# Second attention: the maxima leave from SyncE's queue, the inverse one step later, the last normalisation behind its masks

## What is computed

```python
def _L0_attn_b_ref(encodings, attn_w, attn_b, out_w, out_b):
    qkv = encodings @ attn_w.T + attn_b
    qkv = qkv.reshape(b, n, 16, 3 * 8).transpose(0, 2, 1, 3)
    q, k, v = jnp.split(qkv, 3, axis=-1)
    mask = jnp.arange(n)[:, None] <= jnp.arange(n)[None, :]
    scores = jnp.einsum('bhki,bhqi->bhkq', k, q) / math.sqrt(8)
    scores = jnp.where(mask, scores, -10000.0)
    probs = jax.nn.softmax(scores, axis=2)
    combined = jnp.einsum('bhkq,bhkl->bhql', probs, v)
    out = combined.transpose(0, 2, 1, 3).reshape(b, n, 128)
    return out @ out_w.T + out_b
```

## Time and profile before

| | us |
|---|---|
| median of 3 runs | 768.71 (766.55 to 768.84) |
| the profiled execution, its own time | 768.21 |
| its span, first to last instruction | 766.4 |
| PE busy in the span | 685.7 (89%) |
| DVE, ACT, POOL busy | 484.8, 454.9, 431.0 |
| second attention, block 0 to block 7 | about 348 to 573 |

### The profile page before, as it was taken

One profiled execution on the slowest core, in us unless ns is written; L12 is line 12 of the kernel. 1 busy time (PEld: TensorE's weight loads), 2 busy tenths in 40 slices (PEclk: granted clock), 3 DMA queues, 4 the chain that ended last, 5 costly groups with the idle time before them and its releaser, 6 DMA issues.

```text
span 766.4 us, 13977 instructions
## 1 busy us (share of the span) xinstructions
PE 685.7 (89%) x4706; PEld 472.0 (62%) x4706; DVE 484.8 (63%) x957; ACT 454.9 (59%) x801; POOL 431.0 (56%) x444
## 2 busy tenths in 40 slices
PE   3789896799999999999999999999878899999996
PEld 1455555477787777665555555555445777777784
DVE  6668885567555586456767767766658356675510
ACT  2677774555665565445656566666665555556663
POOL 4455441377867776433444544543555677777763
PEclk9999998899999999999999999999999999999998
DMA  6110320000000003531645654645111000000000
GB/s 182 39 38 20 62 27 2 0 1 1 0 1 0 0 0 99 177 111 43 209 147 177 239 169 156 229 140 180 57 63 41 16 15 15 14 0 15 15 15 27
DMA packets 33028, 52.47 MB, mean 68 GB/s; under 512 B 4560, under 2 KB 9680, under 8 KB 32976
## 3 DMA queue, kind: packets, MB, share of 16 engines
q1 hardware_dynamic: 32784, 51.53, 21.3%
q10 hardware_dynamic: 192, 0.26, 0.1%
HBM read 27.15 MB, written 24.38 MB: 67 GB/s over the span
## 4 chain that ended last, share of the span: by engine, by line
PE 48%; DVE 13%; POOL 13%; issue 12%; ACT 8%; DMA 5%; ACTq 1%; POOLq 1%; DVEq 0%; SPq 0%
PE banks L220 44%; POOL f_h_lo L1122 5%; POOL f_g_lo L1129 5%; ACT b_prob L1448 2%; DMA b_o_dram<-b_o 2%; DVE xn L182 2%; DVE a_mx L645 2%; PE banks L212 2%; ACT a_prob L548 1%; DMA b_den<-b_o_dram 1%; DVE a_prob L657 1%; DVE f_hidden L1072 1%; DVE a_straight L630 1%; PE banks L957 1%; DVE f_gate L1068 1%
## 5 line engine op out<-in xcount | busy, mean ns | idle before, releaser
L1129 POOL TENSOR_TENSOR f_g_lo<-f_gelu,f_g_hi 128x512 fp32r<-128x512 f32 x128 | 167.9, 1316 | 68.8 <-ACT f_g_hi L1024 68.5
L1023 ACT ACTIVATE f_gelu<-banks,cols 128x512 f32<-128x512 f32 x128 | 88.2, 689 | 141.9 <-PE banks L220 139.3
L220 PE MATMUL banks<-f_g_hi,whi 128*128 128x512 f32 x320 | 132.7, 415 | 15.1 <-POOL f_g_lo L1129 15.1
L1534 DVE TENSOR_REDUCE b_segment_max<-banks 128x6 f32<-128x768 f32 x128 | 116.2, 949 | 45.0 <-PE banks L220 44.6
L1644 POOL TENSOR_SCALAR_AFFINE_SELECT b_prob<-b_prob 128x512 f32<-128x512 f32 x128 | 81.7, 641 | 111.6 <-ACT b_prob L1448 111.4
L1448 ACT ACTIVATE b_prob<-banks 128x768 f32<-128x768 f32 x128 | 102.6, 809 | 63.4 <-PE banks L220 55.0
L220 PE MATMUL banks<-f_g_lo,whi 128*128 128x512 f32 x320 | 128.1, 400 | 0.0
L1122 POOL TENSOR_TENSOR f_h_lo<-f_hidden,f_h_hi 128x512 fp32r<-128x512 f32 x60 | 77.5, 1292 | 58.7 <-DVE f_h_hi L1075 58.7
L220 PE MATMUL banks<-f_h_hi,whi 128*128 128x512 f32 x256 | 104.4, 408 | 3.2 <-POOL f_h_lo L1122 2.7
L220 PE MATMUL banks<-f_h_lo,whi 128*128 128x512 f32 x256 | 102.1, 399 | 0.0
L1024 ACT ACTIVATE f_g_hi<-banks,cols 128x512 fp32r<-128x512 f32 x128 | 87.1, 680 | 0.0
(11 more groups left out here) (124 smaller groups left out, 1052.1 us busy)
## 6 DMA issues: line engine op xcount, KB each, us to landing
f_h_hi<-b_q_dram SPq DMA_DIRECT2D x16, 512.0 KB, 4.0
f_h_lo<-b_k_dram SPq DMA_DIRECT2D x16, 512.0 KB, 5.0
b_o_dram<-b_o SPq DMA_DIRECT2D x8, 1024.0 KB, 4.3
b_q_dram<-b_q_hi SPq DMA_DIRECT2D x16, 256.0 KB, 3.2
b_k_dram<-b_k_hi SPq DMA_DIRECT2D x16, 256.0 KB, 3.3
w_stage<-in_wF SPq DMA_DIRECT2D x8, 352.0 KB, 3.2
b_q_dram<-b_q_lo SPq DMA_DIRECT2D x8, 256.0 KB, 3.4
b_k_dram<-b_k_lo SPq DMA_DIRECT2D x8, 256.0 KB, 3.8
```

The source lines that it names most:

```text
L220: return nc.tensor.matmul(out, lhsT, rhs, start=start, stop=stop)
L1023: nc.scalar.activation(gf[c % 2][:, :], z_bank[c % 2], ACT.Gelu, scale=scale).then_inc(s_gf, 1)
L1129: nc.gpsimd.tensor_tensor(lo[:, c, :], gf[c % 2][:, :], hi[:, c, :].bitcast(F32), ALU.subtract).then_inc(s_glo[c % 2], 1)
L1534: nc.vector.reduce_max(seg[:, g, s, 2 * p:2 * p + 2, :], first_pass[:, 2 * p:2 * p + 2, 0:3 * P].rearrange("p b (c k) -> p b c k", c=3), A ...
```

## The change

act_max keeps the negation and loses its two waits and its DMA. SP sends the maxima instead. Those of half 1 of block b go out in sp_out, between the loads of b_oT and b_den and the wait for the inverse (in block 0, which has no sp_out, before sp_rows). Those of half 0 of block b+1 go out in sp_rows, between the loads of half 0 and those of half 1 (in block 6, which has no sp_rows, behind sp_out). The very first go out before block 0. DVE's inverse moves from step 2 to step 3. In block 7 the normalisation of block 6 moves behind all of that block's masks.

```diff
-            INVERSE_AT = 2
+            INVERSE_AT = 3
@@ act_max
                 nc.scalar.activation(nmT[half][:, :], misc[0:2 * GROUPS, :], ACT.Copy, scale=-1.0).then_inc(s_nm, 1)
-                act.wait_ge(s_nm, HALVES * m.t + half + 1)
-                act.wait_ge(s_p1, STEPS * m.t + HALF * (half + 1))
-                act.dma_start(qs[m.odd][3 * DB::QUART, 2 * half:2 * half + 2, :].bitcast(F32), nmT[half][:, :].bitcast(F32))\
-                    .then_inc(s_ml[half][m.odd], 16)
@@ pool_body
-                    if before and n == OUT_AT:
+                    if before and one and n == OUT_AT:
                         pool_normalise(pool, b.after(-1))
...
+                if not one:
+                    pool_normalise(pool, b.after(-1))
@@ sp_rows
                 for half in range(HALVES):
+                    if half and between:
+                        between()
                     if not fresh:
                         sp.wait_ge(s_p2, v["used"][half])
@@
+            def sp_max(sp, m, half, v):
+                sp.wait_ge(s_nm, v["negated"])
+                sp.dma_start(qs[m.odd][3 * DB::QUART, 2 * half:2 * half + 2, :].bitcast(F32), nmT[half][:, :].bitcast(F32))\
+                    .then_inc(s_ml[half][m.odd], 16)
@@ sp_out
                 sp.dma_start(den[:, :], view[:, DB, :].rearrange("h (c t) -> h c t", t=DEN_COLS)).then_inc(s_ol, 16)
+                if between:
+                    between()
                 sp.wait_ge(s_inv, v["read"])
@@ sp_body
                 if before:
-                    sp_out(sp, b.after(-1), out_at)
+                    sp_out(sp, b.after(-1), out_at, send_max)
+                else:
+                    send_max()
                 if two:
-                    sp_rows(sp, b.after(2), rows_at, False)
+                    sp_rows(sp, b.after(2), rows_at, False, send_next_max)
+                elif one:
+                    send_next_max()
```

More of the change, by code:

```diff
@@ L1701, in rows_values, with sp_rows @@
                         "used": [value(sp, UNITS * (n.t - 2) + UNITS // HALVES * (half + 1)) for half in range(HALVES)]}
-            def sp_rows(sp, n, v, fresh):
+            def sp_rows(sp, n, v, fresh, between=None):
                 if not fresh:
@@ L1725, in sp_rows, with max_values @@
                             .then_inc(s_ld[half][n.odd], 16)
+            def max_values(sp, m, half):
+                return {"negated": value(sp, HALVES * m.t + half + 1)}
+            def sp_max(sp, m, half, v):
+                sp.wait_ge(s_nm, v["negated"])
+                sp.dma_start(qs[m.odd][3 * DB::QUART, 2 * half:2 * half + 2, :].bitcast(F32), nmT[half][:, :].bitcast(F32))\
+                    .then_inc(s_ml[half][m.odd], 16)
             def out_values(sp, b):
@@ L1729, in out_values, with sp_out @@
                         "read": value(sp, b.t + 1)}
-            def sp_out(sp, b, v):
+            def sp_out(sp, b, v, between=None):
                 sp.wait_ge(s_oc, v["copied"])
@@ L1748, in sp_body, with send_max, send_next_max @@
                 rows_at = rows_values(sp, b.after(2)) if two else None
+                max1_at = max_values(sp, b, 1)
+                max0_at = max_values(sp, b.after(1), 0) if one else None
+                def send_max():
+                    sp_max(sp, b, 1, max1_at)
+                def send_next_max():
+                    sp_max(sp, b.after(1), 0, max0_at)
                 if before:
-                    sp_out(sp, b.after(-1), out_at)
+                    sp_out(sp, b.after(-1), out_at, send_max)
+                else:
+                    send_max()
                 if two:
-                    sp_rows(sp, b.after(2), rows_at, False)
+                    sp_rows(sp, b.after(2), rows_at, False, send_next_max)
+                elif one:
+                    send_next_max()
             def sp_program(sp):
@@ L1757, in sp_program @@
                     sp_rows(sp, n, rows_values(sp, n), True)
+                sp_max(sp, FIRST_BLOCK, 0, max_values(sp, FIRST_BLOCK, 0))
                 sp_body(sp, FIRST_BLOCK, False, True, True)
```

## The result

The changed kernel takes 778.39 us in the median of four runs (777.32 to 782.86), the kernel before 767.85 (766.55 to 768.84) in the same comparison: a ratio of 1.0156, with a 95% interval of 1.0128 to 1.0183. It is slower, by 10.5 us. The forecast was 770.9, with a range up to 776.0; the time lies outside it.

What follows compares the result with a forecast made beforehand. PE, busy for 89% of the span, was taken as the bound, with SP's chain setting the period after. Blocks -0.7 + 1.8 - 1.8 - 0.7 = -1.4, plus 3.6 for clock falls, gave +2.2: 770.9 us, range 763.5 to 776.

Steps and rivals of the forecast that it cites:

- The freed ACT: Steps 0 and 5: without ACT's DMA issue PE gains 0.45 and 0.80, 1.25 us a block, 29.06 to 27.8.
- The deciding term, SP's chain: Blocks 1 to 5: the later inverse delays the row loads; period 29.4, +1.8 us over five blocks.
- The maxima: Half 0's maxima, sent behind the k load at block starts: 0 to 0.7 us a block, taken as 0.
- The clock: Half clock after PE's waits at starts of blocks 2 to 6: 1.2 us in three of five, +3.6, bounds 0 and 6.
- Blocks 6 and 7: The last two blocks: block 6 loads no rows and gains 1.8 us; block 7 gains 0.7.
- The maxima come last: Rival: PE waits at block starts for maxima, not k rows; 0.4 to 0.7 a block, 773 to 774.4; chance 0.17.
- No clock falls: Rival: same chain, but waits too short or wrongly placed for falls; -1.4, 767.3 us; chance 0.32.
- short chain everywhere: Rival: every block gets block 3's 13.25 us chain; period 28.67, -5.2, 763.5 us; chance 0.10.
- the inverse is hidden: Rival: SP's chain after the inverse is under 12.4 us, so no wait; -9.5, 759.2 us; chance 0.03.
- The normalisation behind the masks: Block 7: masks of step 7 no longer wait behind the normalisation; gain 0.4 us.

Runs made afterwards that it cites:

- e1: The changed kernel with the inverse put back after step 2, SP still sending the maxima and the last normalisation behind its masks: 763.64 us, ratio 0.9937.
- e5: The kernel before with SP sending the maxima and nothing else changed (inverse in step 2, last normalisation ahead of its masks): 762.77 us, ratio 0.996.
- e2: The kernel before with only the inverse moved to step 3, ACT still sending the maxima: 774.49 us, ratio 1.0106.
- e6: The changed kernel with the inverse's store and load on SP between the stores of q and those of k: 764.28 us, ratio 0.9967.
- e3: The changed kernel with the maxima of half 0 sent ahead of both loads of half 0: 778.81 us, ratio 1.0156.
- e9: e5 with the maxima of half 1 sent right behind the issue of the output's store: 762.97 us, ratio 0.9959.
- e10: e9 with the last block's normalisation behind its masks, as in the change: 764.08 us, ratio 0.9972.
- e8: The changed kernel with one extra matmul, its result unused, at the start of step 0 of blocks 1 to 6: 771.91 us, ratio 1.0059.
- e4: The changed kernel with SP holding back the loads of half 1 until the next block's step 0 has made its second scores: 782.49 us, ratio 1.0151.

## Why the prediction was wrong

**The freed ACT: right in kind and about right in size.** 1.25 us a block were forecast, a period of 27.8 without other limits. From first pass to first pass e1 and e5 show 28.0 in the mean of blocks 1 to 5: 27.2 to 27.6 in blocks 2 to 4, and 28.8 to 29.4 in blocks 1 and 5, behind which PE still waits for SP's transfers (in e1 0.7 and 1.0 us).

**The deciding term, SP's chain: right in kind, too small.** The forecast said that PE would wait at each block's start, with the chain through the inverse as the cause. It does, and e2 and e6 show that cause: the inverse alone makes the wait, and taking the stores of q out from behind it removes 14.1 us. From the first pass to the inverse's store I had 13.88. After, it is 13.97 in block 1 and 13.44 in block 5, and 14.9 to 16.2 where the clock fell in between: right. From the inverse's store to the next first pass I had 1.47 + 14.0 + 0.07 = 15.54. After, the five blocks have 17.13, 16.17, 16.08, 15.39 and 16.42, mean 16.24: **0.70 short a block, 3.5 in five**.

Half of the 0.70 is the inverse's own store: in blocks 1 and 5 the load went out 2.56 and 2.19 us behind it, in place of the 1.47 that I used for all, which is 0.36 in the mean of five. From that load to the landing of the k rows it was 14.20 in place of 14.0, and from there to the first pass 0.21 in place of 0.07.

What stands beside the small store where it is slow can be seen in the view of DMA queues. It has one more queue in blocks 1 (386 to 390 us) and 5 (510.9 to 513.1) than in block 2 (418 to 421), where the store took 1.45:

```profile
q8 instruction: 1, 0.02, 2.0%
...
q8 instruction: 1, 0.02, 2.8%
```

That is a transfer of 16 KB on the queue that the profile calls instruction, begun 0.08 and 0.16 us behind the issue of the store. In the 13 traces other than e6 the inverse is stored 104 times. All 15 stores that took over 1.6 us (1.67 to 3.13) had such a transfer under way, and of the 89 that took 1.45 or so, one had, for its first 0.2 us. In e6 the two slowest, 4.05 and 3.88, had one too, and the three at 2.2 to 2.3 had none.

In e2, with ACT as the sender, the mean to the next first pass is 15.78; 0.18 of its 0.24 is the same thing, in one block. Leaving out the slow stores, the change is 0.34 over the forecast and e2 0.06, so by this comparison of two single traces SP's sending of the maxima costs about 0.28 a block. The longer stores have the instruction transfers beside them and aren't counted to it.

**The maxima: the wrong end of a range.** I had 0 to 0.7 a block and took 0, "as they are 16 KB beside 512". The chain shows these 16 KB landing 4.25 us after their issue: size doesn't help behind 1 MB of rows. The measured 0.28 lies below the middle of the range. Of it PE feels about half directly: only in blocks 3 and 6 did it start the first pass later than the k rows' landing allows, by 0.14 and 0.50, which is 0.13 in the mean of five. By e3 it can't be had back by sending them first: then the k rows go out later and come last.

By the rule of the Trainium skill (DMA: Bandwidth & Descriptors, Queues, rings and completion order), that one queue is served in order, the upper end should have held, as the prediction says. The same section adds that a later transfer of a queue may still finish ahead of an earlier one, which the prediction left out. The trace shows both sides: the maxima took 4.25 behind the rows, against 3.4 from ACT's queue, where they were sent at 455.75 in the kernel before with rows under way; but in all five blocks PE went on with them 0.05 to 0.9 us ahead of the landing of the k load that was issued before them.

**The clock: the price was right, the number of falls wasn't. This is the term that failed most.** I took 1.2 us each. The blocks of the change with no fall, one and two falls between first pass and the inverse's store took 13.4 to 14.0, 14.9 to 15.0, and 16.2: 1.2 us each. But I had three falls, at three of the five starts of blocks 2 to 6. They came at four of the five, and at two of these they lasted for two pieces. There are four in the loop, two in block 6 and two more than before in block 7: eight, some 9.6 us in place of 3.6, if those in blocks 6 and 7 cost what those in the loop do, which no run shows apart. The wait that I forecast was 1.6 in the mean; the four waits of blocks 3 to 6 were 1.64 to 2.88 and the first 3.16, since the chain was 0.7 longer and the blocks with a fall came later in their turn. That is the feedback that the sum lacked: a fall delays the inverse, which is at the head of SP's chain, so the next block's rows are late by the same amount, and nothing in the block can win it back.

**Blocks 6 and 7: the forecast gain turned into a loss.** I gave block 6 -1.8, because it loads nothing that could be late. But its maxima, and the rows of block 7 that its first pass reads, were sent in block 5: PE waited 2.88 at its start, and two falls followed. With 2 x 1.2 the sum would have been +0.6; measured is +1.4, and 0.8 of it I can't place. In block 7 I wrote that step 4 "can't use what it gains", and priced that as a gain missed. It was a wait of 1.09 us, and the two falls more; -0.7 + 1.09 + 2.4 = +2.8, measured +2.7.

**The sum again.** Without the clock the forecast was -1.4. Add 3.5 for the chain and 1.1 for block 7, 9.6 for the falls, take off 0.7 for the 0.14 by which the way to the inverse is shorter than forecast once 1.2 is taken off for each fall (13.74), and 1.2 for the fall at 345.7 that only the profiled execution of before had: +10.9. The difference of the spans is 10.8. That it comes out so near is partly luck, since the 0.8 of block 6 and the 0.4 ahead of the second attention are left out and go opposite ways.

**The rivals.** "The maxima come last" shows its sign, as PE's long wait ends with them at each of the five starts, but in three of these the k rows came later still. Its price, 0.4 to 0.7 a block, was above the 0.28 of the runs, and it isn't why the change is slow, as e3 shows. "No clock falls" is contradicted by four falls, "short chain everywhere" by 16.24, "the inverse is hidden" by every block's wait. What no rival held was the two together: waits large enough that the clock falls in most blocks, and the last two blocks pulled in. The range took the clock's upper bound of +6 and the maxima's upper end as alternatives; the waits that bring falls came with late maxima. Even both together would have given 776.8, as the bound of +6 counts five falls and there were eight.

**The normalisation behind the masks** got no price of its own in the runs: e9 and e10 differ by 1.1 us with intervals that overlap almost wholly, e5 and e1 likewise. The 0.4 that I gave it is neither shown nor excluded.

What stays open: whether the instruction transfer holds up the small store, as it is seen beside it in every slow case outside e6, but wasn't moved by any run; why two falls lasted for two pieces and block 5 had none; the 0.8 us of block 6; and how much of e8's 6.5 us is the falls and how much the shorter waits, since its filler moves the starts of the blocks too.

## What to carry to other kernels

When a step is moved in a stream that one engine works through in order, price all that stands behind it up to its next reader, not the step: here a reciprocal of 0.55 us, some 1.5 us later (2.4 with the falls), held back six stores of rows and the four loads behind them. A wait of 1.5 to 3 us at a place where PE was busy throughout is to be counted with a fall of the clock behind it (four of five such waits had one here), and with the next round that it delays. A step that is too early in one round of a loop and too late in another can have its place by round: one condition was worth 4.8 us here, and the same store and load behind three others in SP's queue 14.1.

## What the runs showed of the hardware

A small transfer isn't quick behind large ones on the same queue. The 32 KB of the inverse land after 1.45 us alone, and after 2.2 to 2.3 behind three stores of 256 KB (e6); the 16 KB of the maxima after 4.25 behind two loads of 512 KB; the 1 MB of the output mostly after 4.3, and after 5.7 to 9.3 behind loads of rows (e4).

A small store was slow wherever a transfer of the queue that the profile calls instruction was under way: beside its 16 KB the inverse's store took 1.67 to 3.13 us in place of 1.45 (15 stores), and 3.88 and 4.05 in place of 2.2 to 2.3 behind the stores of q. The runs show that the two coincide, not that or how one delays the other.

In blocks 2 to 6 of the changed kernel, e2 and e9 the granted clock fell to 0.50 (1.2 GHz) behind waits of PE between 1.3 and 3.2 us, and stayed there for 3.4, 6.8 or 10.2 us while PE had work without a gap. The length didn't follow the wait: 1.32 us was followed by 10.2 us at half clock in e9, and 3.16 us by 3.4 in the changed kernel. Nor was a wait always followed by one: e2 waited 0.6 to 1.3 us at four block starts without a fall, and the changed kernel 1.64 and 0.32 at the start of block 5. In e1 a fall of block 6 came behind three short waits, of 0.54, 0.89 and 0.28.
